# The last network of a four-stage kernel as two halves half a cycle apart, with unread products on TensorE

## What is computed

```python
def _coupling_net(h, w1, b1, w2, b2, w3, b3, w4, b4):    # 128 -> 128 -> 64 -> 32 -> 1
    h = _gelu(h @ w1 + b1)
    h = _gelu(h @ w2 + b2)
    h = _gelu(h @ w3 + b3)
    return jax.nn.sigmoid(h @ w4 + b4)
def _twist(x):
    o_r, o_i, p_r, p_i = jnp.split(x, 4, axis=-1)
    return jnp.concatenate([p_r, -p_i, -o_r, o_i], axis=-1)
gf = _global_net(x.mean(axis=1, keepdims=True), ...)     # 128 -> 64 -> 32 -> 1
out = x
for _ in range(NUM_CYCLES):                              # 3
    tf = _coupling_net(out, ...)
    combined = 0.7 * gf + 0.3 * tf
    coupling = BASE_COUPLING + adaptive_range * (combined - 0.5) * 2.0
    out = out + coupling * _twist(out)
```

## Time and profile before

| | us |
|---|---|
| median of 3 runs (979.55 to 981.05) | 979.75 |
| the profiled execution's own time | 980.15 |
| its span in the trace | 978.5 |
| PE busy in the span | 743.9 |
| DVE busy | 753.4 |
| ACT busy | 469.1 |
| last write of DVE to the end of the span | 2.7 |
| mean granted clock of TensorE | 0.885 |

### The profile page before, as it was taken

One profiled execution on the slowest core, in us unless ns is written; L12 is line 12 of the kernel. 1 busy time (PEld: TensorE's weight loads), 2 busy tenths in 40 slices (PEclk: granted clock), 3 DMA queues, 4 the chain that ended last, 5 costly groups with the idle time before them and its releaser, 6 DMA issues.

```text
span 978.5 us, 12306 instructions
## 1 busy us (share of the span) xinstructions
PE 743.9 (76%) x3564; PEld 304.7 (31%) x3564; DVE 753.4 (77%) x1205; ACT 469.1 (48%) x546; POOL 397.7 (41%) x511
## 2 busy tenths in 40 slices
PE   5369999999999999969479962944667667677761
PEld 3212222222222222355357751411222222224311
DVE  3589999999999999555012217788999999998748
ACT  2237777777777777714122322863323323331441
POOL 3525633233322331006705451039977776660000
PEclk9669999999999999957879995956999989899685
DMA  4652221221212223121124313023543434420231
GB/s 123 213 193 54 54 55 52 52 54 52 56 49 55 55 54 95 23 63 33 51 68 121 99 61 86 3 89 141 196 150 135 165 134 151 131 85 0 55 75 43
DMA packets 58774, 83.78 MB, mean 86 GB/s; under 512 B 16787, under 2 KB 35654, under 8 KB 58726
## 3 DMA queue, kind: packets, MB, share of 16 engines
q1 hardware_dynamic: 45794, 66.19, 22.4%
q0 software_dynamic: 9472, 11.09, 4.0%
q10 hardware_dynamic: 3460, 5.89, 1.7%
HBM read 63.58 MB, written 16.16 MB: 81 GB/s over the span
## 4 chain that ended last, share of the span: by engine, by line
PE 39%; DVE 36%; issue 13%; POOL 4%; DMA 4%; ACT 3%; SPq 2%; DVEq 0%; ACTq 0%; POOLq 0%
DVE arena L1007 12%; PE pair L1405 10%; DVE arena L1266 7%; PE pair L1393 7%; PE pair L1484 7%; DVE arena L1260 5%; PE pair L1574 4%; PE pair L1585 4%; POOL slot_x_d L639 3%; DVE xnum L283 1%; SPq L485 1%; DVE ln_stats L271 1%; PE pair L1634 1%; DVE arena L1320 1%; PE pair L1692 1%
## 5 line engine op out<-in xcount | busy, mean ns | idle before, releaser
L1007 DVE TENSOR_REDUCE arena<-pair 128x1 f32<-128x512 f32 x512 | 327.3, 686 | 20.3 <-PE pair L1395 16.0
L749 ACT ACTIVATE arena<-pair 128x1024 f32<-128x1024 f32 x256 | 248.3, 1022 | 95.6 <-PE pair L1405 95.6
L701 POOL TENSOR_TENSOR arena<-arena 128x1024 f32<-128x1024 f32 x64 | 150.0, 2353 | 50.9 <-DVE arena L1260 49.6
L1260 DVE TENSOR_TENSOR_SCAN arena<-pair,arena 128x1024 f32<-128x1024 f32 x64 | 146.2, 2285 | 2.7 <-POOL arena L701 2.7
L903 ACT ACTIVATE pair<-arena,alog 128x1024 f32<-128x1024 f32 x64 | 71.5, 1118 | 149.2 <-DVE arena L1260 149.2
L1692 PE MATMUL pair<-arena,ident 128*128 128x512 f32 x256 | 128.7, 627 | 11.7 <-DVE arena L1272 11.7
L1484 PE MATMUL pair<-arena 128*32 128x512 f32 x1024 | 137.0, 607 | 0.6 <-ACT arena L749 0.6
L1405 PE MATMUL pair<-arena 99*128 99x512 bf16 x512 | 134.8, 386 | 0.1
L1393 PE MATMUL pair<-arena 64*128 64x512 bf16 x256 | 102.8, 402 | 30.7 <-DVE arena L1007 22.7
L1395 PE MATMUL pair<-arena 64*128 64x512 bf16 x256 | 102.9, 402 | 0.0
L1683 PE MATMUL pair<-arena,sel 96*128 96x512 bf16 x128 | 40.9, 403 | 77.0 <-DVE arena L1266 71.3
(11 more groups left out here) (260 smaller groups left out, 938.7 us busy)
## 6 DMA issues: line engine op xcount, KB each, us to landing
arena<-b_rows_d SPq DMA_DIRECT2D x64, 512.0 KB, 3.7
arena<-in_L_ffn_w SPq DMA_DIRECT2D x16, 256.0 KB, 2.9
arena<-q_parts_d SPq DMA_DIRECT2D x32, 96.0 KB
arena<-q_parts_d POOLq DMA_DIRECT2D x32, 96.0 KB, 2.4
arena<-k_parts_d SPq DMA_DIRECT2D x32, 96.0 KB
arena<-xT SPq DMA_DIRECT2D x48, 64.0 KB
slot_x_d<-zero ACTq DMA_DIRECT2D x4, 645.0 KB, 8.7
arena<-slot_x_d SPq DMA_DIRECT2D x8, 322.5 KB, 3.6
```

The source lines that it names most:

```text
L701: g.tensor_tensor(dBu[:, k % HRING, :], du[:, q, :], Bs[:, k % HRING, :], ALU.mult)\
L749: sc.activation(probs[:, kt % NPROB, :], st_pair[kt % 2][:, :], ACT.Exp, scale=SCALE)\
L1007: v.reduce_max(mx[:, mslot, n // 2, n % 2:n % 2 + 1], ring_bank[item % 3], AX).then_inc(s_("ring_read"), 1)
L1260: v.tensor_tensor_scan(hh[:, k % HRING, :], dA_pair[k % 2][:, :], dBu[:, k % HRING, :], 0.0, ALU.mult, ALU.add)\
```

## The change

The four chunks become two halves (`h` = 0, 1: a batch row each) whose steps interleave: PE, ACT and DVE each get a written-out order in which half 1 is about half a cycle behind half 0, and the three cycles are no loop any more. Each half has its own counters (`net_mm{h}`, `net_act{h}`). The twist is two transfers of 256 KB for each half. `tw_s` is gone: the update multiplies tanh, twist and the constant in one operation. The steady term is one operation of 1024 elements for a half, made ahead of the other half's update. In the last cycle, DVE's add-backs of half 0 (with their statistics) stand ahead of half 1's update, and PE's turning back of half 0 ahead of half 1's layer four. The four small operations go ahead of the third layer norm. And PE gets products of bf16 constants, 96 x 384, into columns of a bank that nobody reads (`warm`): eight at the first normed tile, then pairs ahead of certain layers.

```diff
-NET_STEPS = 11
+NET_STEPS = 6
 @block.sync
-                for dst, src in ((0, 64), (32, 96), (64, 0), (96, 32)):
-                    sp.dma_start(tw_in[dst:dst + 32, c, :], xT[src:src + 32, c * CH:(c + 1) * CH])\
-                        .then_inc(s_(f"loaded{c}"), 16)
+            def twist(i, h):
+                sp.wait_ge(s_("state_ready"), NCH * i + 2 * h + 2)
+                for dst, src in ((0, 64), (64, 0)):
+                    sp.dma_start(tw_in[dst:dst + 64, 2 * h:2 * h + 2, :].rearrange("p c n -> p (c n)"),
+                                 xT[src:src + 64, h * L:(h + 1) * L]).then_inc(s_(f"loaded{h}"), 16)
 @block.scalar
+            for i in range(CYCLES):
+                if i > 0:
+                    gelu3(i, 0)
+                gelu1(i, 1, 0)
+                gelu1(i, 1, 1)
+                tanh(i, 0)
+                gelu2(i, 1)
+                if i + 1 < CYCLES:
+                    gelu1(i + 1, 0, 0)
+                gelu3(i, 1)
+                if i + 1 < CYCLES:
+                    gelu1(i + 1, 0, 1)
+                    gelu2(i + 1, 0)
+                tanh(i, 1)
 @block.vector
+            def steady(i, h):
+                dve.wait_ge(s_(f"loaded{h}"), ALL_UNITS + 32 * (i + 1))
+                dve.wait_ge(s_("state_ready"), NCH * i + 2 * h + 2)
+                ch.mark(v.scalar_tensor_tensor(half(base, h), half(tw_in, h), c_in[:, 2, h:h + 1], xT[:, h * L:(h + 1) * L],
+                                               ALU.mult, ALU.add))
+
+            def update(i, h):
+                for k in range(2):
+                    c = 2 * h + k
+                    dve.wait_ge(s_(f"net_act{h}"), NET_STEPS * i + 4 + k + 1)
+                    ch(v.scalar_tensor_tensor(prod[:, c, :], tf[:, c, :], c_in[:, 3, 0:1], tw_in[:, c, :], ALU.mult, ALU.mult))
                     v.tensor_tensor(xT[:, c * CH:(c + 1) * CH], base[:, c, :], prod[:, c, :], ALU.add)\
                         .then_inc(s_("state_ready"), 1)
+            steady(0, 0)
+            for i in range(CYCLES):
+                update(i, 0)
+                steady(i, 1)
+                if i + 1 < CYCLES:
+                    steady(i + 1, 0)
+                else:
+                    add_back(0)
+                    add_back(1)
+                update(i, 1)
+            for gi in range(2, 4):
+                add_back(gi)
+                ln_end(dve, v, ch, 4 * gi - 8, 4, 12 + gi - 1, "x4_ready")
+            for gi in range(2, 4):
+                ln_end(dve, v, ch, 4 * gi, 4, 12 + gi + 1, "x4_ready")
 @block.tensor
+            def warm(n):
+                for _ in range(n):
+                    t.matmul(bank[7][:, CH // 4:CH], ident_b[0:96, :], sel[:, 0:3, :].rearrange("p s n -> p (s n)"),
+                             start=True, stop=True)
+
+            pe.wait_ge(s_("x3_ready"), 1)
+            warm(8)
...
+            for i in range(CYCLES):
+                if i > 0:
+                    warm(2)
+                    layer3(i, 0)
+                layer1(i, 1, 0)
+                layer1(i, 1, 1)
+                layer4(i, 0)
+                warm(2)
+                layer2(i, 1)
+                warm(2)
+                if i + 1 < CYCLES:
+                    layer1(i + 1, 0, 0)
+                layer3(i, 1)
+                if i + 1 < CYCLES:
+                    layer1(i + 1, 0, 1)
+                    warm(2)
+                    layer2(i + 1, 0)
+                else:
+                    back(0)
+                    back(1)
+                layer4(i, 1)
+            back(2)
+            back(3)
```

More of the change, by code:

```diff
@@ L920, in global_act @@
                 sc.activation(dst, src, function, bias=bias, scale=scale).then_inc(s_("global_act"), 1)
[L922 to L943, removed]
@@ L945, in _, with gelu1, gelu2 @@
-            cycle(0, True)
-            with act.Fori(1, CYCLES) as i:
-                cycle(i, False)
+            def gelu1(i, h, k):
+                act.wait_ge(s_(f"net_mm{h}"), NET_STEPS * i + k + 1)
+                sc.activation(m1[:, 2 * h + k, :], bank[2 * h + k][:, :], ACT.Gelu, bias=biasT[:, CNB1_ROW:CNB1_ROW + 1])\
+                    .then_inc(s_(f"net_act{h}"), 1)
+            def gelu2(i, h):
+                act.wait_ge(s_(f"net_mm{h}"), NET_STEPS * i + 3)
+                sc.activation(m2[:, h, :], bank[4 + h][:, :], ACT.Gelu, bias=cb2[:, :]).then_inc(s_(f"net_act{h}"), 1)
@@ new lines, in gelu3, with tanh @@
+            def gelu3(i, h):
+                rows = slice(64 * h, 64 * h + 64)
+                act.wait_ge(s_(f"net_mm{h}"), NET_STEPS * i + 4)
+                sc.activation(m3[rows, :], bank[6][rows, :], ACT.Gelu, bias=cb3[rows, :]).then_inc(s_(f"net_act{h}"), 1)
+            def tanh(i, h):
+                for k in range(2):
+                    act.wait_ge(s_(f"net_mm{h}"), NET_STEPS * i + 4 + k + 1)
+                    act.wait_ge(s_("state_ready"), NCH * i + 2 * h + 2)
+                    sc.activation(tf[:, 2 * h + k, :], bank[2 * h + k][:, :], ACT.Tanh, bias=cb4[:, :], scale=0.5)\
+                        .then_inc(s_(f"net_act{h}"), 1)
@@ L1331, in _, with add_back @@
-            with dve.Fori(1, CYCLES) as i:
-                cycle(i, False)
-            for gi in range(4):
+            def add_back(gi):
                 dve.wait_ge(s_("back_done"), gi + 1)
@@ L1758, in _, with layer1, layer2 @@
-            cycle(0, True)
-            with pe.Fori(1, CYCLES) as i:
-                cycle(i, False)
-            pe.wait_ge(s_("net_act"), NET_STEPS * CYCLES)
-            for c in range(NCH):
+            def layer1(i, h, k):
+                c = 2 * h + k
+                pe.wait_ge(s_("state_ready"), NCH * i + c + 1)
+                t.matmul(bank[c][:, :], cw1[:, :], xT[:, c * CH:(c + 1) * CH], start=True, stop=True)\
+                    .then_inc(s_(f"net_mm{h}"), 1)
+            def layer2(i, h):
+                for k in range(2):
+                    pe.wait_ge(s_(f"net_act{h}"), NET_STEPS * i + k + 1)
+                    last = t.matmul(bank[4 + h][64 * k:64 * k + 64, :], cw2[:, :], m1[:, 2 * h + k, :], start=True, stop=True)
+                last.then_inc(s_(f"net_mm{h}"), 1)
@@ L1763, in _, with back @@
+            def back(c):
                 pe.wait_ge(s_("state_ready"), NCH * CYCLES + c + 1)
```

101 lines of the change are left out of this document (42 added, 59 removed).

## The result

The changed kernel takes 975.88 us in the median (973.34 to 977.54), the kernel before 979.75 (977.82 to 981.7), in seven runs each. The ratio is 0.9962, 95% interval 0.995 to 0.9975: 3.7 us faster. The profiled execution took 977.54 us; its span is 975.9 us, and 1.6 us lie around it, as before.

A forecast was written before the change was run, and what follows sets the result against it. It took twist transfers, 10.2 + 2.0 us, then about 4 us of DVE, to bound each cycle, and DVE the end. Add-backs 4.2 plus pipeline 0.4 made -4.6 us: 975.2 us against the 979.75 median, range 973.0 to 979.0.

The forecast's parts named there:

- Start: Before the network: four small DVE operations ahead of the layer norm delay the first layer-one product by 0.62 us.
- First cycle: First network cycle: half 1 written at 933.8 us, ending 3.7 us later than before, half 0 far into its second.
- ring: Each cycle after the first: a chain through both halves in PE's queue order, 13.87 us against 16.3 and 16.1.
- The transfers: Twist in each cycle: a half's pair lands 3.5 us after its state, bounds 2.7 to 4.3, at worst 6.9.
- limit of 3.84: In the cycles: the twist is hidden up to 3.84 us after its state; each us beyond costs one per cycle.
- Rival 1: Twist transfers land late, each us past the hidden time costing one per cycle: 976.5 to 981 us, chance 0.09.
- End: After the last cycle: last update 958.9 to 961.8 us, then 9.4 us of DVE against 13.5, ending at 971.2.
- Clock: PE in the network: full clock from the second layer-two product to the last layer four, held by unread bf16 products.
- rivals 2 and 3: PE's clock falls once per cycle, 977.8 to 979 us (chance 0.11); or never rises in the network, 998 us (0.06).
- Sum: Whole kernel: -4.6 us, 4.2 from two add-backs filling DVE's wait and 0.4 from the pipeline of halves.
- The pipeline of halves: Network cycles: two shorter cycles and an earlier tanh, less the start and the first cycle's trailing half, bring 0.4 us.
- The replay: The prediction's hand-made list of each engine's operations in the changed order, with the trace's durations and handovers.

The follow-up runs named there:

- the small transfers: The changed kernel with four transfers of 32 partitions per chunk instead of two of 64 per half: 977.04 us, ratio 0.998 to the kernel before.
- large transfers: The kernel before with only the twist edited, two transfers of 64 partitions per half instead of four of 32 per chunk: 973.71 us, ratio 0.995.
- in phase: The changed kernel with both halves in step, add-backs behind the last update and no unread products: 972.08 us, ratio 0.9928 to the kernel before.
- forms alone, with small transfers: The kernel with both halves in step and no unread products, with four transfers of 32 partitions per chunk: 975.04 us, ratio 0.9967 to the kernel before.

## Why the prediction was right, and where it was not

The number was right (975.2 for 975.88, range 973.0 to 979.0), and so was, within half a microsecond at each point, the forecast schedule. Its account of what causes the gain was wrong; that the number held in spite of it is no luck, since it was read off the schedule and not off that account. Point by point:

- **Start.** The four small operations stand where said, and the first layer-one product comes 16.44 us after the mixer's addition (913.18 - 896.74) for 15.81 before (910.94 - 895.13): 0.63 later, forecast 0.62.
- **First cycle** and **ring.** From layer one to the end of half 1's first update 22.55 us, forecast 22.3; the ring 14.21 us, forecast 13.87. The 0.34 us is in PE's handovers: a layer-one product with another layer's group behind it holds PE for 1.06 us (935.79 to 936.85), not 0.86, the wait behind layer three is 0.7 us for 0.46, and layer two takes 1.0 for 0.86; shorter links give some 0.2 back.
- **The transfers.** Landing was mis-sized, 4.24 us for 3.5, though inside the bounds of 2.7 and 4.3 that the rows gave. By the prediction's own limit of 3.84 that would have cost 0.4 us per cycle; since the ring was longer too, the limit measures about 4.2, and what is exposed is under 0.05 us. Either miss alone gives a ring of 14.2 to 14.3 us; that they overlap and do not add is luck. Rival 1's rule is confirmed by the small transfers. The prediction's estimate of 3.2 us for the pair, from the fixed cost and rate of the Trainium skill ("DMA: Bandwidth & Descriptors", "Anatomy of one DMA"; its fit is for transfers that GpSimd issues), was 0.5 short of the 3.72 from the second issue. The Trainium skill's rule that transfers to disjoint partition halves serialize ("DMA: Bandwidth & Descriptors", "Rules for kernel authors") stays open: no run here moved one half alone.
- **End.** The last update ends 2.86 us after it begins, and 9.20 us of DVE follow (964.00 to 973.20); forecast 2.88 and 9.4.
- **Clock.** Full from 916.25 to 960.6 us, about as forecast, but not by the unread products; rivals 2 and 3 are refuted even without them. A pair of those held PE 0.43 us (937.91 to 938.34), not 0.32, off the ring. The Trainium skill's warning about clock swings from frequent small idles ("TensorE: Matmul & The Clock Gate", "A second HAM failure mode: psum-queue depth-cycling") does not come true in these runs: pauses in PE's work of 0.3 to 1.3 us stand in rows at 1.00.
- **Sum: the step that failed.** "Of the gain 4.2 us are the two add-backs that fill DVE", "The pipeline of halves brings 0.4 by itself". Measured, in steps that each have their own run:

| step | stretch us | worth |
|---|---|---|
| before | 80.68 | |
| large transfers | 76.00 | -4.68 |
| fused product, steady terms of 1024, small operations moved, no loop (in phase) | 73.80 | -2.20 |
| halves half a cycle apart, with the unread products | 77.86 | +4.06 |
| add-backs ahead of the last update | 76.46 | -1.40 |

As a place in time the sum came true: the gain stands behind the last write. As a cause it did not: the add-backs are worth a third of what they were given. The prediction had the numbers for that: its tanh was ready at 956.2 and its last update began at 958.9, so 2.7 us of the 4.2 were paid at once; it booked the filled time as a gain and that delay as part of the halves' account. And "the pipeline" was one entry for three things of opposite sign. The transfers and the forms would have given 6.9 us by themselves, and the offset takes 4.1 of that back. The replay compared the new order with the old kernel only, never with the new transfers in the old order. The row that told it was on the table: half 1's products wait in PE's queue behind half 0's, and the ring was written down as a sum through both halves.

What the decomposition does not settle: the order of the steps matters (forms alone, with small transfers, gave 4.2 us; transfers alone 4.7; both 6.9), and the second step's parts were not run apart. In each of these three, 0.3 to 0.4 us lie ahead of the first write of the state, where the moment of the clock's rise differs from execution to execution; the offset's price of 4.1 may be too high by 0.3 for the same reason.

## What to carry to other kernels

When a change bundles a relief (fewer issues on a queue) with a new order, replay the relief in the old order as well. Once the transfers no longer bound this cycle, four chunks in step were a shorter ring than two halves half a cycle apart, because engines that take their queues in order make each half wait for the other's late data. Work put into a wait is worth the wait's length, not its own: subtract how far it puts off what follows it. And where medians scatter with work ahead of the edit, measure a stretch between two fixed operations, and look for what still moves inside it: here it repeats within 0.03 us in the changed order, while a clock that rises earlier or later moves it by up to 0.4 us in the others.

## What the runs showed of the hardware

- Issuing an on-chip transfer took SP 0.6 us, at 64 KB as at 256 KB, so 16 of them are 10.2 us of queue. Instructions of the issuing line, of before (64 KB) and of after (256 KB): duration ns, min/median/max:
```profile
L485 SPq DMA_DIRECT2D arena<-xT x48: 507/591/1855, 904.7 to 951.8; - x48
```
```profile
L486 SPq DMA_DIRECT2D arena<-xT x12: 461/572/1145, 910.3 to 950.5; - x12
```
  The pair of 256 KB landed 3.72 us after its second issue began; the last of a row of 64 KB transfers 2.0 us after its issue began.
- TensorE's granted clock fell to 0.50 in a wait of some 4 us and was back at 1.00 within the next layers. In the kernel before that cost 0.2 us of the second cycle, in phase 0.9.
- The moment of the rise in the first cycle differed between profiled executions with the same products ahead of it: on the chain the four layer ones took 5.26 and 4.83 us in one pair of kernels, 4.94 and 4.64 in another.
- A layer-one product with another of layer one behind it held PE 0.86 us (the two activations that read a pair start at 921.89 and 922.75), with another layer's group behind it 1.06. Whether the 0.2 us comes of the other shape or of the other weights, no run here shows.
